# One graph layer on one core: ten merges spread over two stages, a weight table written row by row, Gram columns and node tiles in another order

## The reference, cut to what matters

```python
xn = _layernorm(x)
# graph attention over the edges
h = xn @ W;  al = h @ a_l;  ar = h @ a_r
e = exp(-leaky_relu(al[src] + ar[dst], 0.1))
h_prime = segment_sum(e[:, None] * h[dst], src) / (segment_sum(e, src) + eps)
# linear attention
query = (xn @ w_query_left) * (xn @ w_query_right)
kv = (xn @ w_key).T @ (xn @ w_value)
x = x + elu(h_prime) + query @ kv
# experts: softmax gate, the best 2 of 8, weights w
x = x + sum_e comb[:, e] * (_layernorm(x) @ expert_W[e] + expert_b[e]) / 2
```

## Time and profile before

| | us |
|---|---|
| median of 3 runs | 1205.07 |
| lowest and highest | 1201.33, 1205.38 |
| the profiled execution | 1205.13 |
| its span | 1203.0 |
| TensorE busy | 1152.0 (96%) |
| VectorE busy | 592.4 (49%) |
| GpSimd busy | 464.0 (39%) |
| ScalarE busy | 308.5 (26%) |
| mean granted TensorE clock | 0.979 |

### The profile page before, as it was taken

The page is one execution under the profiler, slowest core; times in us unless marked ns, Lnnn a source line. Parts: engine busy times, 40 slices in busy tenths (PEclk is TensorE's granted clock), DMA queues, the critical chain, the costliest instruction groups (busy, mean ns, idle before and its releaser), DMA issues.

```text
span 1203.0 us, 15119 instructions
## 1 busy us (share of the span) xinstructions
PE 1152.0 (96%) x5588; PEld 986.7 (82%) x5588; DVE 592.4 (49%) x1171; ACT 308.5 (26%) x416; POOL 464.0 (39%) x394
## 2 busy tenths in 40 slices
PE   6999999999999999989999999999957999999996
PEld 5898888888788999989988878888846888788884
DVE  7935666655332122201123357997589722644444
ACT  2421212133120211102021213343253411523232
POOL 0003457467787577700000016223322443434343
PEclk9999999999999999999999999999967999999998
DMA  9282785863634444592066643463287955785753
GB/s 359 105 342 52 204 226 123 247 173 42 132 44 43 92 92 111 117 224 81 29 185 200 212 149 109 158 253 130 94 296 262 360 88 94 239 250 120 194 86 72
DMA packets 115835, 192.15 MB, mean 160 GB/s; under 512 B 33960, under 2 KB 63912, under 8 KB 114624
## 3 DMA queue, kind: packets, MB, share of 16 engines
q1 hardware_dynamic: 81008, 159.53, 38.4%
q0 software_dynamic: 34768, 31.82, 19.0%
HBM read 136.19 MB, written 61.68 MB: 164 GB/s over the span
## 4 chain that ended last, share of the span: by engine, by line
PE 85%; DVE 10%; DMA 3%; issue 1%; ACT 1%; POOL 0%; DVEq 0%; ACTq 0%; POOLq 0%
PE ps L1558 27%; PE ps L1559 27%; PE ps L1560 27%; DMA q_in<-in_L_mix_w_query_right 2%; DVE e_lo L1383 2%; PE ps L1775 2%; PE ps L1644 1%; DVE xn_lo L1110 1%; DVE stats L1082 1%; PE ps L1704 1%; DVE tok_w L1497 1%; DVE acc L1098 1%; PE ps L1604 1%; DVE y L1528 0%; ACT lt_hi L1006 0%
## 5 line engine op out<-in xcount | busy, mean ns | idle before, releaser
L729 POOL DMA_INDIRECT cnt_d<-times,addr_i x160 | 264.7, 1655 | 178.0 <-DMA cnt_d<-times,addr_i 93.4
L1558 PE MATMUL ps<-e_hi,lt_hi 128*128 128x512 f32 x368 | 148.0, 402 | 2.9 <-DVE e_lo L1383 2.3
L1560 PE MATMUL ps<-e_hi,lt_lo 128*128 128x512 f32 x368 | 144.0, 391 | 0.0
L1559 PE MATMUL ps<-e_lo,lt_hi 128*128 128x512 f32 x368 | 143.9, 391 | 0.0
L1558 PE MATMUL ps<-xt_hi,q_hi 128*128 128x416 f32 (+1 forms) x384 | 136.1, 354 | 4.9 <-DVE q_lo L1217 4.9
L1559 PE MATMUL ps<-xt_lo,q_hi 128*128 128x416 f32 (+1 forms) x384 | 136.0, 354 | 0.0
L1560 PE MATMUL ps<-xt_hi,q_lo 128*128 128x416 f32 (+1 forms) x384 | 135.5, 353 | 0.0
L836 POOL DMA_INDIRECT out<-y,row_put x46 | 73.7, 1601 | 89.0 <-ACT y L1040 50.3
L747 POOL TENSOR_TENSOR att_part<-att 128x640 f32<-128x640 f32 x10 | 15.8, 1580 | 220.4 <-PE ps L1560 207.0
L1558 PEld LDWEIGHTS ps<-e_hi,lt_hi 128*128 128x128 f32 x368 | 69.5, 189 | 23.3 <-DVE e_lo L1383 9.2
L1560 PEld LDWEIGHTS ps<-e_hi,lt_lo 128*128 128x128 f32 x368 | 69.4, 189 | 14.8
(11 more groups left out here) (257 smaller groups left out, 2391.3 us busy)
## 6 DMA issues: line engine op xcount, KB each, us to landing
e_raw<-in_L_ffn_expert_W SPq DMA_DIRECT2D x64, 512.0 KB, 10.1
cnt_d<-zeros SPq DMA_DIRECT2D x20, 640.0 KB, 13.3
rows<-key_d SPq DMA_DIRECT2D x8, 1250.0 KB, 8.0
acc<-in_x SPq DMA_DIRECT2D x18, 512.0 KB, 6.7
w_raw<-in_L_mix_w_key SPq DMA_DIRECT2D x16, 512.0 KB, 4.1
cnt_d<-cnt_d POOLq DMA_DIRECT2D x10, 640.0 KB, 19.3
cnt<-cnt_d SPq DMA_DIRECT2D x10, 640.0 KB, 6.0
h_d<-hs SPq DMA_DIRECT2D x18, 256.0 KB, 2.0
```

The source lines that it names most:

```text
L729: nc.gpsimd.indirect_dma_start(out=cnt_d[i], out_offset=bass.IndirectOffsetOnAxis(ap=addr_i[:, j:j + 1], axis=0), in_=times[:, j:j + 1], i ...
L1558: nc.tensor.matmul(o, lh, rh, start=(k == 0), stop=False)
L1559: nc.tensor.matmul(o, lh, rl, start=False, stop=False)
L1560: return nc.tensor.matmul(o, ll, rh, start=False, stop=(k == last_k))
```

## The change

Four things are changed.

- GpSimd waits before each of the ten merges: merge t for the first group of query unit 9 + t, and the last three for the first half of mix tiles 0, 1 and 2.
- The three products for `tok_w` run over rows (p, t, s) with s innermost: the output is written in runs of 29 elements, `tok_s` is read with a step, and the weight is repeated along s. Behind them both `block_lo` of block 0 stand ahead of the four `expert_lo`.
- `T` makes the Gram columns 7, 6, ... 0 (`T_ORDER`), the copies go to the matching places, and `KV` takes its inner blocks in that order. Before the first job TensorE waits for the copies of the Gram pieces only, and for those of the last lower blocks one job later.
- `XT_FIRST` begins with (0, 0), and (0, 1) is fourth instead of sixth.

```diff
+    MERGE_Q = 7
...
+        T_ORDER = list(range(KB))[::-1]
...
-        XT_FIRST = [(6, 0), (7, 0), (0, 0), (6, 1), (7, 1), (0, 1), (1, 0), (1, 1), (2, 0), (2, 1)]
+        XT_FIRST = [(0, 0), (6, 0), (7, 0), (0, 1), (6, 1), (7, 1), (1, 0), (1, 1), (2, 0), (2, 1)]
...
             for t in range(NT):
+                n = NQ - MERGE_Q + t
+                pool.wait_ge(s_full, 1 + (q_job(n, 0) if n < NQ else mix_job(n - NQ, 0)))
...
-                    evac(first[f"T{h}"] + m, t_hi[:, m, :])
+                    evac(first[f"T{h}"] + m, t_hi[:, T_ORDER[m], :])
...
-                    evac_lo(n, t_lo[:, m, :], ps[:, n % NB, :], t_hi[:, m, :])
+                    evac_lo(n, t_lo[:, T_ORDER[m], :], ps[:, n % NB, :], t_hi[:, T_ORDER[m], :])
...
-                    if t == XT_ORDER[0] and g == 1:
+                    if (t, g) == (XT_FIRST[0][0], 1):
...
-                last = V.tensor_tensor(tok_w[:, :, j, :].rearrange("p t s -> p s t"), tok_s[:, :, :], over_slots(w_part[:, j, :]), ALU.mult)
+                last = V.tensor_tensor(tok_w[:, :, j, :], tok_s[:, :, :].rearrange("p s t -> p t s"),
+                                       w_part[:, j, :].unsqueeze(2).to_broadcast([P, 2 * NT, NSLOT]), ALU.mult)
...
-            block_lo(0, 0)
-            expert_lo(0, range(FIRST_LO, MB + 1))
-            block_lo(0, 1)
-            expert_lo(0, range(MB + 1, KB))
+            for g in range(2):
+                block_lo(0, g)
+            expert_lo(0, range(FIRST_LO, KB))
...
                 if h == 0:
-                    pe.wait_ge(*released(first["T0"] - 1))
-                    pe.wait_ge(*released(first["T0"] - 2))
-                for m in range(KB):
-                    n = first[f"T{h}"] + m
+                    pe.wait_ge(*released(first["LOW"] - 1))
+                for j, m in enumerate(T_ORDER):
+                    n = first[f"T{h}"] + j
+                    if h == 0 and j == 1:
+                        for x in (1, 2):
+                            pe.wait_ge(*released(first["T0"] - x))
...
-                    for k in range(KB):
+                    for j, k in enumerate(T_ORDER):
                         if m == 0:
-                            pe.wait_ge(*released(first[f"T{h}"] + k))
+                            pe.wait_ge(*released(first[f"T{h}"] + j))
```

More of the change, by code:

```diff
@@ L1634, in _ @@
                     col = (m % MB) * P
-                    for k in range(KB):
+                    for j, k in enumerate(T_ORDER):
                         if m == 0:
-                            pe.wait_ge(*released(first[f"T{h}"] + k))
+                            pe.wait_ge(*released(first[f"T{h}"] + j))
                         last = three(ps[:, n % NB, :], w_hi[c % 2][:, k, col:col + P], w_lo[c % 2][:, k, col:col + P],
-                                     t_hi[:, k, :], t_lo[:, k, :], k, KB - 1)
+                                     t_hi[:, k, :], t_lo[:, k, :], j, KB - 1)
                     last.then_inc(s_full, 1)
```

## The result

The changed kernel takes 1197.51 us (median of 6 runs, 1195.34 to 1201.76) against 1205.22 us of the kernel before beside it (6 runs, 1201.33 to 1208.68). The ratio is 0.9945, with a 95% interval of 0.992 to 0.997: faster by 7.7 us in the medians, where 11.2 us were forecast. A second measurement on another chip, with its own runs of the kernel before, gave 1195.95 us and 0.9916 [0.9899, 0.9934]. In microseconds the first interval is 3.6 to 9.6 and the second 8.0 to 12.2, so the forecast of 11.2 lies outside the one and inside the other. The kernel before varies by itself, by 5 to 10 us from run to run; the experiments show part of the reason.

What follows compares the result with a forecast made beforehand. TensorE, busy 96% of the span, was taken as the bound, so only its gaps could be won. Gains of 5.1 (7.5 - 2.4), 4.3, 0.9 and 0.9 sum to 11.2 us: 1205.1 to 1193.9 us, range 1190.0 to 1198.5.

Steps and rivals of the forecast that it cites:

- the signs that were to show it wrong: Query stage still loses time, the three table products take over 5 us, or TensorE stands before the attention stage.
- Part 1, the query stage: Units 9 to 15: pacing the merges wins back the whole 7.53 us lost to the burst.
- Part 1, merge 6: Before the first mix tile: merge delays the last store by 2.4 us (bounds 0 and 3.4), making the stall 3.0.
- rival B: Before the mix: store gets through ahead of merge 6, which then meets only waiting time; 1191.5 us, chance 0.11.
- Part 1, the clock: Before the mix: TensorE's clock stays up through the 3.0 us stall; a fall, 2.64 us, left for the range.
- Rival A: Before the mix: stall lowers the clock, 3.4 + 2.64 = 6.0 us given back; 1197.5 us, chance 0.13.
- Part 1, merges 7 to 9: Mix stage: lag of 3.4 us or less each is worked off before attention; cost 0, bounds 0 and 3 us.
- rival E: Mix stage: residual loop never catches up, 9.3 us stall before attention plus 2.64 for the clock; 1209.5 us, chance 0.03.
- Part 2: Weight table in routing: three products fall from 8.00 to 3.0 us; second gather limits the gain to 4.3 us.
- rival C: Weight table: stepped reads are as slow as stepped writes, so nothing is gained there; 1198.2 us, chance 0.06.
- Parts 3 and 4: Gram columns and node tile order: waits before 87.19 and 266.70 us go, 0.9 us each, bounds 0.8 and 1.0.
- D: Query stage: burst isn't the cause or pacing doesn't spread it, 7.5 us stay; 1199.0 us, no separate chance given.

Runs made afterwards that it cites:

- first profile: Profiled execution of the changed kernel in the first measurement, the slowest of its six runs: 1201.76 us, span 1199.7.
- second profile: Profile of the same changed kernel from the second measurement, on another chip: span 1195.3 us; median there 1195.95 us, ratio 0.9916.
- the last experiment: Version with all ten merges in the query stage, SyncE also waiting for the second gather before expert 2's weights: 1195.47 us, 0.9932 of the kernel before.

## Why the prediction was right and wrong

**What bounds the kernel**: right. The four gaps that were named are gone, and what was won and lost lies on TensorE's path. Of the signs that were to show it wrong, one came: TensorE stands before the attention stage.

**Part 1, the query stage**: right in this pair of profiles, 9.36 us for parts 1, 3 and 4 against 9.3. Its weakness is that 7.53 us stands on one execution. The other bursts lost 6.4, 6.2 and 2.2 us. A load that is caught by a transfer started at a moment that varies has a price that varies too, and the sum took one draw of it for the value.

**Part 1, merge 6**: the size was nearly right (2.8 and 2.6 us, forecast 2.4), the mechanism was not, so the size is luck. The text let two or three of the store's packets through and the other six wait for packets of the merge. The whole store got through first (2.55 against 2.54 us), which was rival B's condition; but then the merge didn't meet only waiting time, it held the load behind the store, by 2.8 us. The Trainium skill's page "DMA: Bandwidth & Descriptors" (Queues, rings and completion order), by which an engine drains a whole packet of one queue before it turns to the next, was read as a wait of the store. The store had passed, so its rows test nothing of it. From 593.0 to 595.5 the merge's packets moved alone while the load was under way, five or so on each engine; whether they are one packet of the page's kind the rows can't tell.

**Part 1, the clock**: wrong. "3.0 lies between, and I keep it up" was the first step that failed: the fallen clock was put at nothing. A stall of 3.0 to 3.4 us did lower the clock in all four profiles that have it before the mix (3.43, 3.25, 3.43 and 3.02 us), and cost 1.6 to 2.9 us more. Rival A, which had the mechanism, stood at 0.13, and its price of 2.64 us was near.

**Part 1, merges 7 to 9**: "I cost them at 0" was the second step that failed. One lag that is worked off in six additions was taken to mean that any lag is. But the count loads at tiles 5 and later come on top of the merges' lag before it is worked off, and the rate at which it shrinks, 0.5 to 1.5 us per addition at the end and nothing in the middle (first profile: 6.5, 6.7, 6.8 us at the 13th to 15th, then 6.1, 5.5, 4.0 and 3.3), leaves 2 to 3 us at the end. That is the loop of rival E, with a stall of 1.18 and 3.69 us where that one had 9.3; the bounds of 0 and 3 us held one profile (1.18) and missed the other (3.69).

**Part 2**: right, step by step. The three products took 3.38 us (forecast 3.0), TensorE was next with its transposes and weight matmuls, and then the second gather ended the wait as forecast, 8.73 us after its issue. 4.77 and 4.08 us were won against 4.3 (by its own rows, 918.54 - 914.1, it would have been 4.4). Of the 4.77, 4.41 come ahead of the first expert matmul. Behind it the clock, which was already up (0.39 us a matmul, against 0.63 in the kernel before), gives another 1.05, which the forecast left out, and the gather's wait takes 0.69 of that. The rule of the Trainium skill's page "SBUF — State Buffer" (Door 1: The DMA port swizzle), that each step to a new line of 16 bytes pays, would have left the table at 8 us: the measured 1.18 us for 580 elements read 40 bytes apart, against 2.77 to 3.00 written 174 bytes apart, decides against it for the read, and rival C is out. What part of the 1.18 us the stepped read takes isn't shown.

**Parts 3 and 4**: right; both waits are gone, and unit 9 comes 1.8 to 2.5 us earlier, for 1.8 forecast. The 2.6 us [0.4, 4.9] of the total can't be laid to them alone: the burst cost their profile 2.2 us where it cost the kernel before 7.5.

**Rivals**: B's price and D are out (there is a stall, and the query stage is even). A is what happened before the mix, plus a small E before attention. The stall, the clock and the second wait come to 9.4 us in the first profile and 5.6 in the second, where 2.4 were forecast; the shortfalls are 7.9 and 3.5. What is left of them, 0.9 and 0.3 us, is 1.52 and 0.73 us in the attention stage less what the other stretches won beyond the forecast. Of the 1.52 us, 1.42 lie ahead of the last attention matmul and are the fallen clock at the stage's start (0.50, then 0.77). The 0.73 lie nearly all in the gate's products at its end, where the clock's fall varies from execution to execution.

## What to carry to other kernels

Spreading a burst is only half of pacing: each piece has to be checked against the chain of store, load and split that has no slack at that moment, and against every loop that can't catch up. Here putting all ten ahead of unit 15 won 4.2 us in the medians over the change (3.0 by the ratios), where the pacing as written gave nothing by itself. A stall on TensorE of 3 us is to be costed with the clock; in this kernel that made it half again to nearly double its length. A gap that depends on when a transfer happens to start should be priced from several executions, not from the one in the profile.

## What the runs showed of the hardware

**VectorE and GpSimd can block each other whole, and the first to start wins.** In the first profile of the change GpSimd's sum started at 714.47, h_lo at 715.35, and h_lo took 2.55 us instead of 1.22, ending 1.07 us after the sum. The kernel with five merges in the mix shows the same 2.55. In the second profile of the change h_lo came first and the sum paid (timeline of VectorE and GpSimd):

```profile
712.33 1.22 DVE L1302 TENSOR_TENSOR h_lo<-h_in,h_hi 98x1024 fp32r<-98x1024 f32 x1
712.62 2.35 POOL L751 TENSOR_TENSOR att_part<-att 128x640 f32<-128x640 f32 x1 [80.76 <-PE ps L1564]
```

Undisturbed the sum takes 1.57. The sum's own 2.36 us in the first profile fit this too: `att_lo` had started ahead of it, at 713.95. So a lag that puts the split behind the start of the sum costs 1.3 us on top: that is the rest of the 3.69 us, and in the kernel with five merges in the mix it is the rest of the 4.09 (3.7 - 0.87 + 1.33 = 4.16). Not every pair does this. An addition with one of its inputs in PSUM ran at full speed beside GpSimd (first profile):

```profile
716.90 1.60 POOL L753 TENSOR_TENSOR att_part<-att_part 128x256 f32<-128x256 f32 x1
717.83 0.68 DVE L1311 TENSOR_TENSOR xm<-ps,xm 98x512 f32<-98x512 f32 x1
```

The Trainium skill's page "SBUF — State Buffer" (SBUF: two separate sides) says it so: the port pair that the two share is a lock, held for a whole instruction by whichever starts first, and a VectorE instruction with two inputs in SBUF takes part in it against a GpSimd one that reads SBUF. The trace agrees: 2.55 against 1.22 us for the split, which has two such inputs, and an unchanged 0.68 us for the addition, which has one.

**A merge and a small load.** A merge moves 640 KB within device memory. Beside one, the load of a mix tile took 6.9 us (3.8 without merges), and a residual tile of 256 KB 8.1 us. A store issued 0.35 us after a merge was through ahead of it and lost at most some tenths, since the merge's data began to move only 1.8 to 1.9 us after its issue; a store issued 4.9 us after one took 2.9 us instead of 2.1.

**The clock and stalls.** It fell in each stall of 3.0 us or more in the query and mix stages (3.02, 3.25, 3.43, 3.69, 4.09 and, with a burst, 4.55 to 4.89), and in none of 0.6 to 1.9 us there. Among the experts it fell in the one of 2.77. It fell without a stall as well, at the end of the attention stage, in the profile of the last experiment for one (0.78 from 865 to 870), while TensorE was busy with the gate's products of 8 columns.
